# Macaron block (FFN, attention, FFN): the engines' order within a batch of attention laid out anew, TensorE without its loop

## The reference, cut to what matters

```
x: (8, 1024, 128) f32
x = x + 0.5 * ffn(layernorm(x))            # 128 -> 384 -> 128, silu gate, int weights / 127
x = x + attn(layernorm(x))                 # attn returns its own input + gate * out
x = x + 0.5 * ffn(layernorm(x))

attn(y): h = rmsnorm(y) * norm_w
         q, k, v = h@Wq (4 heads of 32), h@Wk, h@Wv (2 heads each, shared by two query heads)
         q, k = q/|q|, k/|k|
         p = softmax(exp(log_temperature) * q k^T, causal)
         return y + gate * (p v) @ Wo
```

## Time and profile before

| | us |
|---|---|
| median of 3 runs | 443.08 (442.51 to 443.92) |
| the profiled execution, its own time | 444.12 |
| its span, first to last instruction | 442.3 |
| first FFN, until the first exponential | about 103 |
| attention, 8 batches | about 103 to 359 |
| second FFN and the last stores | about 359 to 442 |
| mean granted TensorE clock | 0.988 |

### The profile page before, as it was taken

One profiled execution on the slowest core, in us unless ns is written; L12 is line 12 of the kernel. 1 busy time (PEld: TensorE's weight loads), 2 busy tenths in 40 slices (PEclk: granted clock), 3 DMA queues, 4 the chain that ended last, 5 costly groups with the idle time before them and its releaser, 6 DMA issues.

```text
span 442.3 us, 12788 instructions
## 1 busy us (share of the span) xinstructions
PE 400.9 (91%) x4899; PEld 215.4 (49%) x4899; DVE 355.6 (80%) x943; ACT 371.2 (84%) x497; POOL 255.9 (58%) x325
## 2 busy tenths in 40 slices
PE   0689998989896999996999999999999999999994
PEld 0346565664442534533535535435445345676654
DVE  5989997799799796996696996996967958888654
ACT  3899999776896798895799899898988999999950
POOL 5789999984626414634334624633132558999850
PEclk9999999999999899998899999999999999999999
DMA  6586443416236028037009127046052115465442
GB/s 166 128 172 154 50 61 61 95 23 109 64 66 118 11 51 138 9 73 124 1 10 149 37 40 153 4 73 122 1 95 52 25 25 87 105 127 115 110 105 76
DMA packets 119230, 35.21 MB, mean 80 GB/s; under 512 B 101632, under 2 KB 119168, under 8 KB 119168
## 3 DMA queue, kind: packets, MB, share of 16 engines
q1 hardware_dynamic: 117888, 34.02, 40.3%
q10 hardware_dynamic: 1280, 0.33, 0.3%
HBM read 4.98 MB, written 4.19 MB: 21 GB/s over the span
## 4 chain that ended last, share of the span: by engine, by line
PE 54%; DVE 12%; ACT 11%; issue 7%; POOL 7%; DMA 7%; SPq 1%; ACTq 0%; DVEq 0%
PE ps L724 11%; PE ps L507 10%; PE ps L754 9%; PE ps L761 9%; ACT PT L867 4%; PE ps L787 4%; PE ps L571 4%; PE ps L560 3%; DMA AXT<-AS 3%; ACT XN L459 3%; DVE H L328 2%; PE ps L731 2%; PE ps L596 2%; POOL HL L434 2%; DVE RD L241 1%
## 5 line engine op out<-in xcount | busy, mean ns | idle before, releaser
L867 ACT ACTIVATE PT<-ps,k_exp 128x1024 f32<-128x1024 f32 x144 | 154.0, 1125 | 13.7 <-PE ps L731 11.2
L507 PE MATMUL ps<-XT,WT 128*128 128x512 f16 x384 | 94.1, 384 | 6.0 <-DMA XT<-w_int 2.1
L724 PE MATMUL ps<-QKT 128*32 128x512 f16 (+1 forms) x1280 | 90.3, 364 | 9.3 <-issue 4.4
L754 PE MATMUL ps<-PT,V 128*32 128x512 f32 (+3 forms) x768 | 77.6, 495 | 0.0
L761 PE MATMUL ps<-PT,ones 128*32 128x512 f32 (+3 forms) x768 | 76.0, 486 | 0.0
L434 POOL TENSOR_TENSOR HL<-H,HH 128x1024 f16<-128x1024 f32 x31 | 66.5, 2146 | 8.1 <-ACT HH L483 5.3
L328 DVE SCALAR_TENSOR_TENSOR H<-SG,k_isilu,ps 128x1536 f32<-128x1536 f32 x32 | 57.9, 1808 | 13.9 <-ACT SG L477 5.7
L999 POOL TENSOR_TENSOR ST<-QN,ST 128x512 f16<-128x512 f32 x16 | 19.3, 1208 | 71.5 <-ACT ST L899 71.5
L507 PEld LDWEIGHTS ps<-XT,WT 128*128 128x128 f16 x384 | 34.5, 98 | 50.6 <-issue 11.5
L724 PEld LDWEIGHTS ps<-QKT 128*32 128x32 f16 x1280 | 29.5, 96 | 56.2 <-ACT PT L867 26.9
L459 ACT ACTIVATE XN<-X,NB,RS 128x128 f32<-128x128 f32 x128 | 52.4, 483 | 3.1 <-POOL NB L406 3.0
(11 more groups left out here) (139 smaller groups left out, 660.2 us busy)
## 6 DMA issues: line engine op xcount, KB each, us to landing
result<-X SPq DMA_DIRECT2D x15, 256.0 KB, 2.5
X<-in_L_attn_x SPq DMA_DIRECT2D x7, 512.0 KB, 4.3
X<-in_L_attn_x SPq DMA_DIRECT2D x2, 256.0 KB, 4.7
XT<-w_int SPq DMA_TRANSPOSE x32, 3.1
QKT<-ST SPq DMA_TRANSPOSE x18, 5.9
AXT<-AS SPq DMA_TRANSPOSE x16, 2.9
w_int<-in_L_ffn_w_gate SPq DMA_DIRECT2D x1, 192.0 KB, 4.2
w_int<-in_L_ffn_w_up SPq DMA_DIRECT2D x1, 192.0 KB, 4.4
```

Of the source, the lines that this page charges most:

```text
L507: i = e.matmul(out[:, j, :], WT[:, wp, w * NJ + j, :], XT[k % 2][:, xp, :], start=a == 0, stop=a == len(passes) - 1)
L724: i_ = e.matmul(dst[r, :].rearrange("p (s a n) -> p s a n", a=2, n=P), QKT[k % 2][:, i // TPC, NH + hp, key0 + r.start:key0 + r.stop], q.r ...
L754: e.matmul(sums_of(h, 0, n), V[k % 2][:, i, v0:v0 + HD], weights_of(g, h, o, n), start=i == 0, stop=i >= TPC * qc, skip_group_check=True)
L867: e.activation(dst, SCORES[(SLOT0[g] + i) % 2][:, :, :], ACT.Exp, scale=k_exp[:, 0:1]).then_inc(a_exp, 1)
```

## The change

TensorE's attention step is written out for all eight batches (when `shift` is false). SyncE turns x between the two stack turns of a batch. The second half of the last projections and the output projection of the batch before move one group later; ScalarE's extras get other groups; VectorE computes statistics at the end of the batch before, splits the two `normalise`, and moves `wo_out` and `add_norm`; GpSimd does both `rstds` first and `stack_lo` of half 1 last. No instruction that computes is added or removed.

```diff
--- before.py
+++ after.py
@@ -614,10 +614,10 @@
-        USES = {0: [("qkv", 0, 0), ("qkv", 0, 1)], 1: [("qkv", 1, 0), ("qkv", 1, 1)],
-                2: [("wo", 1)], 7: [("rows", 0)], 9: [("wo", 0), ("rows", 1)]}
-
-        MOVED = {0: [], 1: [], 2: USES[0], 3: USES[1]}
+        USES = {0: [("qkv", 0, 0), ("qkv", 0, 1)], 1: [("qkv", 1, 0)], 2: [("qkv", 1, 1)],
+                3: [("wo", 1)], 7: [("rows", 0)], 9: [("wo", 0), ("rows", 1)]}
+
+        MOVED = {0: [], 1: [], 2: USES[0], 3: USES[1] + USES[2]}
         FIRST = [("qkv", h, c) for h in range(2) for c in range(2)] + [("rows", 0)]
         LATE = [("rows", 1)]
@@ -846,7 +846,11 @@
                         e.wait_ge(s_res, NC)
                     for u in uses_in(k, g):
                         use(k, b, u)
-            drive(e, step, B, 1, 3)
+            if shift:
+                drive(e, step, B, 1, 3)
+            else:
+                for k in range(B):
+                    step(k, k)
         def projections_read(e, shift):
@@ -932,7 +936,7 @@
                         exps(k + 1, b + 1, 0)
                     if g == 1 and k >= 1:
                         o_hi(e, b * 2 - 1)
-                    if g == 8:
+                    if g == 6:
                         o_hi(e, b * 2)
                     if k == B - 1 and g in HEAD:
                         ffn_act(e, 1, [("normalise", HEAD[g])])
@@ -941,18 +945,18 @@
                     if k + 1 < B:
                         if k == 0 and g in (0, 1):
                             x_hi(2 + g, g)
-                        g_ = g - 2 if k == 0 else g
-                        if g_ == 0:
+                        if g == (2 if k == 0 else 0):
                             qkv_out(k + 1, m0, k, b, 0)
-                        elif g_ == 1:
-                            for c in range(2):
+                        for c, at in enumerate((3, 3) if k == 0 else (1, 2)):
+                            if g == at:
                                 v_out(k + 1, m0 + 1, k, b, 1, c)
-                        if g == (4 if k == 0 else G0):
+                        if g == 4:
+                            stack_hi(m0, 0)
+                        if g == 5:
                             squares(k + 1, m0 + 1, k, b, 1)
-                        for half, at in enumerate((4, 6) if k else (5, 7)):
-                            if g == at:
-                                stack_hi(m0 + half, half)
-                    if k + 2 < B and g == NG - 2:
+                        if g == 8:
+                            stack_hi(m0 + 1, 1)
+                    if k + 2 < B and g == 7:
                         x_hi(m0 + 2, 0)
                         x_hi(m0 + 3, 1)
             drive(e, step, B, 1, 3)
@@ -1016,20 +1020,20 @@
                 q = 2 * (k % 2)
                 if later:
                     rstds(m0 + 2, q)
+                    rstds(m0 + 3, q + 1)
                 if k >= 1:
                     o_lo(e, b * 2 - 1)
                 if not nxt:
                     ffn_pool(e, 1, [("rstd", 0), ("x_hi", 0), ("x_lo", 0), ("rstd", 2),
                                     ("x_hi", 1), ("x_lo", 1)])
-                if later:
-                    rstds(m0 + 3, q + 1)
                 if nxt:
                     stack_lo(m0, 0)
-                    stack_lo(m0 + 1, 1)
                 o_lo(e, b * 2)
                 if later:
                     x_lo(m0 + 2, 0)
                     x_lo(m0 + 3, 1)
+                if nxt:
+                    stack_lo(m0 + 1, 1)
                 if not nxt:
                     ffn_pool(e, 1, [("x_hi", 2), ("x_lo", 2), ("rstd", 4)])
             drive(e, step, B, 1, 3)
@@ -1212,41 +1216,46 @@
                 nxt = k + 1 < B
                 later = k + 2 < B
                 q = 2 * (k % 2)
-                if later:
+                if k == 0:
                     stats(m0 + 2, m0 + 2, q)
+                    stats(m0 + 3, m0 + 3, q + 1)
                 if k >= 1:
                     o_norm(e, b * 2 - 1)
                 if not nxt:
                     ffn_dve(e, 1, [("moments", c) for c in range(4)])
-                if later:
-                    stats(m0 + 3, m0 + 3, q + 1)
+                if later and k >= 1:
+                    normalise(m0 + 2, m0 + 2, q)
                 if nxt:
                     sums(m0, 0)
                     norms(20 * b + 20, 4 * b + 6, 0, 1)
                     unit(k + 1, 20 * b + 30, m0, 0)
+                o_norm(e, b * 2, k == 0)
+                if k == 0:
+                    stack_hi2(m0, 0)
+                    normalise(m0 + 2, m0 + 2, q)
+                if later:
+                    normalise(m0 + 3, m0 + 3, q + 1)
                 if k >= 1:
                     wo_out(k, b, ("wo", 1), b * 2 - 1)
-                o_norm(e, b * 2, k == 0)
+                if nxt and k >= 1:
+                    stack_hi2(m0, 0)
                 if nxt:
                     sums(m0 + 1, 1)
-                    stack_hi2(m0, 0)
                     norms(20 * b + 30, 4 * b + 8, 1, 2)
                     unit(k + 1, 20 * b + 40, m0 + 1, 1)
                 if later:
-                    normalise(m0 + 2, m0 + 2, q)
-                    normalise(m0 + 3, m0 + 3, q + 1)
-                if nxt:
-                    stack_hi2(m0 + 1, 1)
+                    add_norm(m0 + 2, m0 + 2, q)
+                    add_norm(m0 + 3, m0 + 3, q + 1)
                 if nxt:
                     rows(m0, k, b, 0)
+                    stack_hi2(m0 + 1, 1)
+                if k + 3 < B:
+                    stats(m0 + 4, m0 + 4, 2 - q)
+                    stats(m0 + 5, m0 + 5, 3 - q)
                 if not nxt:
                     ffn_dve(e, 1, [("moments", c) for c in range(4, NE)])
                 if nxt:
                     wo_out(k, b, ("wo", 0), b * 2)
-                if later:
-                    add_norm(m0 + 2, m0 + 2, q)
-                    add_norm(m0 + 3, m0 + 3, q + 1)
-                if nxt:
                     rows(m0 + 1, k, b, 1)
             drive(e, step, B, 1, 3)
             last_pv_out(e)
@@ -1305,11 +1314,14 @@
                     stack(m, 0, NH, d_u[m % 2])
             for k in range(B):
-                for half in range(2):
-                    qk(2 * k + half)
+                qk(2 * k)
+                if k == 0:
+                    qk(1)
                 for half in range(2):
                     if k + 1 < B:
                         turn_x(e, 2 * k + 2 + half)
+                if k:
+                    qk(2 * k + 1)
         on_all = [[0, P], [1, 1]]
```

## The result

The changed kernel takes **436.12 us** (435.78 to 436.85), 0.984 of the kernel before (0.9824 to 0.9864): 7.0 us faster, where 14.5 were forecast. The direction was right, the size half; the time lies just above the range (435.5). The profiled execution takes 436.85, its span is 435.0 against 442.3. It is the slowest of the four runs (436.85 against 435.78 to 436.20), so a comparison of spans with it can be about 1 us off; the medians are given beside it where this matters.

A forecast was written before the change was run, and what follows sets the result against it. TensorE was taken as the bound, with batches costing more where it waits. The terms 6.56 + 4.43 + 1.63 + 1.0 + 1.2 - 0.3 = 14.5 us, off 443.08, gave 428.6 us, range 424.0 to 435.5.

The forecast's parts named there:

- The loop: TensorE's jump back in attention: straight code removes a 4.39 us stall and 2.17 us of slow clock, 6.56 us.
- x ahead of the second stack: SP's queue: x turned earlier ends TensorE's AXT waits, 4.43 us, and batch 1's slow clock, 1.63 us.
- The second stack: Now made later by ScalarE, it just lands before the fourth group's scores; batch 1 may lose +0.3 us (0 to 1.5).
- rival B: The second stack lands too late for its scores in most batches: 4.8 us lost in all, 433.4 us; chance 13%.
- The start of batch 1: ScalarE no longer waits for x there, so TensorE's 1.22 us wait goes: -1.2 us (bounds 0 and -2).
- rival C: VectorE becomes the bound, normalise held by GpSimd; sign: ScalarE waits for QN before the second stack; 456.6 us, chance 4%.
- ScalarE's spread: ScalarE's same instructions laid one per group: 0.2 us less a batch over five batches, -1.0 us (+2 to -2.5).
- the last batch: OH stands earlier in the last batch: taken at 0, bounded by +0.3 and -1 us.
- VectorE's statistics "cost nothing": Two sets at a batch's end, about 2.4 us, fit VectorE's 4.15 us idle before the output projection's result.
- OH no longer holds ScalarE: VectorE's first reciprocal of a batch starts at once, so OH stops delaying ScalarE early in the batch; no size given.
- A: The loop stall stays on TensorE or moves to another engine's jump: 6.56 us return, 435.2 us; chance 8%.
- D: No effect: ScalarE, at 26.86 of 30 us, sets the pace and removed waits reappear for exponentials; 443 us, chance 2%.

The follow-up runs named there:

- the loop alone: The kernel before with TensorE's attention step written out straight and nothing else changed: 440.00 us, 0.988 of the kernel before.
- with batch 0 kept: Changed kernel with TensorE's extras back in their old groups and VectorE's other order in batches 1 to 7, batch 0's VectorE as changed: 430.47 us.
- two single edits on VectorE: Changed kernel with VectorE either reading the output projection ahead of the statistics (436.83 us) or doing add_norm at the batch's very end (437.94 us).
- the new order: The changed kernel with TensorE's loop put back: 440.02 us, 0.987 of the kernel before.

## Why the prediction was off by half

**The loop** (6.56 us with its clock): right. There is no idle from "issue" over 1 us in the changed kernel's attention, and the clock stays up. That it pays in full only together with x is shown by the run with the loop alone, whose waits for AXT sum to 7.5 us over batches 1 to 5, where the kernel before had 4.43.

**x ahead of the second stack** (4.43 + 1.63): right. No wait for AXT is left and no slow stretch in batch 1; x goes out at T - 3.1 (197.32), where the forecast had T - 1.8. No run takes this term by itself, so its size rests on the waits that are gone. The run with SyncE's old order shows the place in the queue to be a condition of the new ScalarE order, not an extra.

**The second stack** (-0.3, rival B): held. In batches 1 to 7 no scores waited for it, though SyncE issues it at 201.67, T + 1.2, and not at T - 0.3: in batch 2 the eight add_norm steps stood ahead of VectorE's part of it (`stack_hi2`). Its reader came later too, at T + 8.5 (208.94) and not T + 7.7. The one wait for QKT in these batches is for a first stack, ahead of T of batch 5, and the repeat of the kernel does not have it:

```profile
261.12 0.61 PE L724 MATMUL ps<-QKT 128*32 128x512 f16 x8 [0.53 <-DMA QKT<-ST]
```

**The start of batch 1** (-1.2): 1.05 came, but more than half of it by luck. The first row is of the kernel before, the others of the changed one:

```profile
133.80 0.62 PE L724 MATMUL ps<-QKT 128*32 128x512 f16 x8 [0.63 <-DMA QKT<-ST]
```

```profile
136.87 0.51 PE L724 MATMUL ps<-QKT 128*32 128x512 f16 x8 [0.79 <-ACT PT L871]
```

```profile
134.97 0.84 ACT L903 ACTIVATE ST<-QN 128x768 f16<-128x768 f32 x1 [2.14 <-DVE QN L1140]
```

Of the wait of 1.22 us that was to go, 0.43 went; 0.63 is a wait for the first stack that the prediction did not name. The exponentials are late because ScalarE waits 2.14 us for the second norms of batch 0 (0.58 before). That was rival C's sign, but it shows in batch 0 only.

**The first failed step: the projections that moved were counted as slack and not as work in the way.** The prediction took the half projection behind the fourth group's scores only as 0.7 us less for the second stack, did not price the output projection's place, and took "values and sums now stand together before the fifth group's exponentials" inside the bounds of the spread. The half projection carries its copy with it, in front of the copies of values and sums; TensorE meets those 0.45 us early. And the output projection now parts the weighing from the next scores, and ScalarE, busy 27.8 of 31.5 us, loses 0.94 to 1.02 us a batch. Undoing this gives 5.8 us of span: 4.0 in batches 1 to 5, 1.4 in the last two (where the sum had nothing), 0.45 before (of which the repeat of the changed kernel has 0.2 too, so this part may be scatter). In the sum's terms, ScalarE's spread was taken at -1.0 with +2 as its bound and came out at about +3 with these 4.0 us in it; the last batch was taken at 0 with +0.3 as its bound and lost 1.16 (25.36 to 26.52). With it undone a gain of the spread's size appears in batch 6, which had no wait to lose: 30.04 us, before 30.36, where 0.2 a batch was forecast.

**The second: VectorE's statistics "cost nothing".** I placed them in the 4.15 us of idle and left out what else the diff puts there: two add_norm sets beside GpSimd's o_lo, x_lo and stack work. They grow from 375 to 616 ns an instruction over the whole run, the idle is full before the statistics begin, and the reading is late. "The next use of that bank is a projection 3 us on" was right by the trace, and was no cover: the reading came at T + 3.7, and behind it stand the reciprocal and OH, which still holds ScalarE for 0.5 to 0.6 us in each of batches 1 to 5, against "OH no longer holds ScalarE". By itself mending it gives 1.4 us of span (it costs 1.7 at the start of batch 1), and on top of the projections, with batch 0 kept, 1.2 more: 428.0 against 429.19.

With both mended, batches 1 to 5 take 152.85 us where the sum had 152.41, 30.57 each, and the span is 428.0 where it had 427.8. By the profiled executions the missing 7.2 us is what the terms did not count: 5.8 of it the first step, 1.2 the second. The agreement is partly luck: batch 1 takes 1.6 us more than the 30.5 forecast, batches 2 to 5 together 1.2 less. By the medians the miss is 7.5 us, 4.4 of it the first step and 1.3 the second; the best median, 430.47, stays 1.9 above the forecast, and no run says why. The two ways of counting differ because the profiled execution of the kernel before was 1.04 us above its median, and that of the best kernel 0.67 below.

**The rivals.** A is refuted by the absence of any gap at a jump, B's sign, waits for the second stack, never came. D's mechanism, ScalarE setting the pace, is half the story of the first failed step: not by its load but by 1 us of waiting in the wrong place. C named the right pair of engines and the wrong instruction: normalise fell from 489 to 446 ns, add_norm rose from 375 to 616, and the 2.9 us that this cost in batch 2 (5.08 against 2.18) stayed under the 5.3 from which C decides. The Trainium skill (SBUF — State Buffer, Who interferes with whom) says that a tensor_scalar in a two-port mode and a GpSimd operation shut each other out. The trace agrees that they hold each other: 2.9 us for eight steps, 0.36 each, where the shortest of GpSimd's operations beside them takes 0.67. Whether one always waits out the other's whole instruction it doesn't show.

What stays open: batch 1 of the best run still takes 32.11 us. TensorE's waits in it, for X (0.73), exponentials (0.43) and QKT (0.18), are 1.3 us of the 2.0 by which it is longer than each of batches 3 to 6. ScalarE waits there for the norms of q and k (1.90 us), as in batch 0; that the late second norms of batch 0 are the cause of it all is argued and not shown. How the copy of V and the output projection share the 4.0 us of batches 1 to 5 is known only from the copy's side (3.2), as the output projection alone wasn't moved back.

## What to carry to other kernels

When work moves to "after" something on the bounding engine, price it twice: by what then comes earlier and meets an engine that isn't ready, and by who waits for what it now stands in front of. An idle stretch can be spent once only; list everything that the change puts in it, at the duration it has beside the neighbours it will get. Here lateness decided before load did: two single edits on VectorE moved the wait to the next result, and only an order that had all of them on time shortened the batch.

## What the runs showed of the hardware that I had not expected

The jump back on TensorE cost 4.39 us idle in the old order and 2.83 in the new one, at the same place in the program; no run shows why the two differ. One add_norm instruction takes 0.27 us by itself (2.18 for eight) and 0.64 beside GpSimd's two-input operations (5.08 for eight). With the loop alone, the clock is at its lower level behind a wait of 2.41 us for x (granted clock 0.55 from 144.49 to 148.00 us, 2.72 us for twelve matmuls) and at its upper one behind a wait of 2.08 (1.00 from 178.42 to 182.00, 1.47 us). The length of the wait alone doesn't decide it: behind the stall of 2.83 us in the new order the granted clock is 1.00 as well (204.28 to 207.40), behind the one of 4.39 it is 0.58 (208.63 to 213.93).
